# Expert stages of a hybrid convolution and attention network: GpSimd waits after every eighth indirect transfer instead of every fourth

## The chip, the cores and the metric

The kernel runs on one core of a Trainium2 chip. The metric is the device time of one launch in microseconds (us), the median of several runs. A core has five engines that run their own instruction streams and meet at semaphores: TensorE (PE, matrix products), VectorE (DVE), ScalarE (ACT), GpSimd (POOL) and SyncE (SP, here a queue for plain transfers). Sixteen DMA engines move data between the core's memory and the chip's main memory.

## What is computed

Eight images of 128 channels and 32x32 pixels, 8192 tokens of 128 numbers, pass through six layers: convolutional attention, whitening, linear attention, a mixture of experts with GELU, windowed attention, and a mixture of experts with SiLU. The change touches the two mixtures. Both pick two of eight experts for each token:

```python
def _L2_ffn_ref(x, Wr, br, ln_g, ln_b, W1, b1, W2, b2):      # "gelu"
    logits = xt @ Wr + br
    top_p, top_idx = jax.lax.top_k(jax.nn.softmax(logits, axis=-1), 2)
    weights = top_p / top_p.sum(axis=-1, keepdims=True)
    ...                                   # xe: normalised xt, scaled for each expert
    h = jax.nn.gelu(jnp.einsum('end,edh->enh', xe, W1) + b1[:, None, :], approximate=False)
    y = jnp.einsum('enh,ehd->end', h, W2) + b2[:, None, :]
    ...                                   # sel: the two chosen experts' rows of y
    out = (weights[:, :, None] * sel).sum(axis=1)

def _L3_ffn_ref(x, router_w, w1, w2, w3):                     # "silu"
    ...                                   # gates: the two largest probabilities, normalised
    h = jax.nn.silu(h1) * h3              # h1 = flat @ w1, h3 = flat @ w3, for each expert
    out = jnp.einsum('ne,nec->nc', gates, jnp.einsum('neh,ech->nec', h, w2))

t = t + _L2_ffn_ref(_ln_t(t), ...)
t = t + _L3_attn_ref(_ln_t(t), ...)
t = t + _L3_ffn_ref(_ln_t(t), ...)
```

## The kernel before

The layers run one after another, with a barrier of all engines between them. `tokens` (128 partitions x 64 tiles x 128) stays in the core's memory the whole time. A tile is 128 tokens.

A mixture is done in two parts. `route` scores the tokens, picks their two experts and gives each of the 64 x 128 x 2 token copies a row number (`places`), so that in main memory the rows of one expert stand together. `run_experts` (L1358) then moves the rows and multiplies them; it is called once with the prefix `g`/`gx` (gelu) and once with `s`/`sx` (silu).

The tiles are cut into four groups of 8, 24, 24 and 8 (`GROUP_TILES`). Each group has its own buffers in main memory and is sorted by itself into units of 256 rows, 15, 31, 31 and 15 of them (`GROUP_UNITS`), 92 in all. Four streams work on them:

- GpSimd first sends all four groups, then fetches all four (L1437 to L1440). `send_group` (L1413) issues, for each tile, two indirect transfers of 128 rows of 512 bytes each from `normed` to `sorted_rows` (L1416). `fetch_group` (L1422) waits until the group's results are stored, and then fetches parts of four tiles (`SEND`), eight indirect transfers each (L1430), into one of two buffers `fetch`. Counted through, there are 16 parts, numbered 0 to 15: parts 0 and 1 belong to group 0, 2 to 7 to group 1, 8 to 13 to group 2, and 14 and 15 to group 3. From the third part on, it waits before a part until VectorE has added the part two before it (`fetch_used`).
- SyncE loads a unit into `xq` (L1450) and stores a result `yq` (L1456). Before the first unit of a group it waits for all the group's sends: `sp.wait_ge(sent[g], 2 * GROUP_TILES[g] * 16)`.
- TensorE, ScalarE and VectorE run in steps, one unit per step and 96 steps in all: transpose of unit s (`turned`, L1496), first product of unit s-2 (`up`, L1471 to L1473), second product of unit s-4 (`down`, L1506). VectorE copies the weights of the unit's expert into `w_now` in each step (a cast, L1557).
- VectorE adds the fetched rows to `tokens` (`add_result`, L1587 to L1594): tiles of parts 0 and 1 in steps 50 to 57, those of parts 2 to 7 in steps 62 to 85, one tile a step, and the tiles of parts 8 to 15 after the last step. Before the first tile of a part it waits until the whole part has landed (`fetched`).

The order is fixed by the code; no planner is involved. A wait that GpSimd makes holds back everything behind it in its stream. The next layer's instructions follow a barrier that comes after the last addition.

## Time and profile before

| what | value |
|---|---|
| median of 3 runs | 1896.82 us (1893.26 to 1902.1) |
| the profiled execution | 1900.54 us |
| its span, first to last instruction | 1898.8 us |
| TensorE busy | 1268.0 us, 67% |
| VectorE busy | 1126.8 us, 59% |
| GpSimd busy | 807.7 us, 43% |
| GpSimd L1416, sends, 256 transfers | 142.5 us busy (silu) and 128.1 us (gelu) |
| GpSimd L1430, fetches, 256 transfers | 134.8 us busy (silu) and 124.2 us (gelu) |

Busy shares are averages over layers with different limits; what one layer waits for is read in its own stretch. A busy entry of GpSimd for an indirect transfer is the time in which the engine writes the transfer's descriptors; the move itself happens afterwards. The number in brackets behind a row in order of time is how long the engine had been idle, with what released it. In the gelu mixture `run_experts` lies between 572 and 1077 us of the span, in the silu mixture between 1384 and 1878 us.

### The profile page before, as it was taken

What the parts mean: (1) busy time and instruction counts of PE and PEld (TensorE: products, weight loads), DVE (VectorE), ACT (ScalarE), POOL (GpSimd) and SP (SyncE); (2) the same over time, 40 slices, a digit from 0 to 9 for tenths busy, and PEclk for the clock granted to TensorE, in tenths of its full rate; (3) what the DMA queues carried; (4) which work ended last, traced back from release to release, by engine and by line L of the source; (5) the groups of instructions that cost most, each with busy time, mean ns of one, the idle gap of its engine ahead of it and who ended that gap; (6) DMA issues with size and microseconds to landing.
All of it is one profiled execution on the core that took longest, in us unless ns stands there. A gap on an engine that the chain in (4) does not pass through costs nothing. (4 is left out here: it accounts for less than half of the span.)

```text
span 1898.8 us, 34652 instructions
## 1 busy us (share of the span) xinstructions
PE 1268.0 (67%) x12312; PEld 1135.5 (60%) x12312; DVE 1126.8 (59%) x2515; ACT 581.8 (31%) x1223; POOL 807.7 (43%) x717
## 2 busy tenths in 40 slices
PE   3878877356742769899980067766528599999702
PEld 2656557356732768898980045545518599999702
DVE  3999984998761323445541376855626277888612
ACT  2666651021211324445440042324102133333201
POOL 4666650222505655523535410104056666445353
PEclk9899997689556979999995578965559799999956
DMA  9100000000202233323321100003012233333212
GB/s 358 40 18 22 1 1 3 3 1 9 92 0 67 73 101 107 101 88 95 104 73 40 34 2 4 4 3 89 0 56 77 92 108 109 101 99 103 67 39 111
DMA packets 90575, 118.34 MB, mean 62 GB/s; under 512 B 18882, under 2 KB 74170, under 8 KB 90426
## 3 DMA queue, kind: packets, MB, share of 16 engines
q1 hardware_dynamic: 70842, 70.66, 11.8%
q0 software_dynamic: 19584, 45.65, 7.5%
q8 instruction: 99, 1.62, 0.4%
q14 instruction: 50, 0.41, 0.1%
HBM read 59.10 MB, written 57.15 MB: 61 GB/s over the span
## 5 line engine op out<-in xcount | busy, mean ns | idle before, releaser
L199 POOL TENSOR_TENSOR probs_low<-probs,probs_high 128x1024 fp32r<-128x1024 f32 x64 | 152.6, 2387 | 111.2 <-ACT probs_high L387 111.2
L1430 POOL DMA_INDIRECT gx_fetch<-sorted_results,g_places x128 | 124.2, 970 | 164.5 <-DVE tokens L1594 87.3
L1416 POOL DMA_INDIRECT sorted_rows<-s_normed,s_places x128 | 142.5, 1113 | 119.7 <-DMA sorted_rows<-s_normed,s_places 49.6
L1430 POOL DMA_INDIRECT sx_fetch<-sorted_results,s_places x128 | 134.8, 1053 | 134.1 <-DMA sx_fetch<-sorted_results,s_places 51.9
L1506 PE MATMUL gx_down<-g_w_down,gx_hT 128*128 x1472 | 183.6, 279 | 0.2 <-issue 0.2
L1416 POOL DMA_INDIRECT sorted_rows<-g_normed,g_places x128 | 128.1, 1001 | 125.7 <-DMA sorted_rows<-g_normed,g_places 55.0
L1506 PEld LDWEIGHTS gx_down<-g_w_down,gx_hT 128*128 128x128 f32 x1472 | 175.8, 196 | 0.8 <-issue 0.6
L1531 ACT ACTIVATE gx_hT<-gx_up,gx_b_now 128x256 f32<-128x256 f32 x368 | 144.1, 483 | 3.6 <-PE gx_down L1506 3.6
L1506 PE MATMUL sx_down<-s_w_down,sx_hT 128*128 x1104 | 140.6, 277 | 3.6 <-issue 2.1
L1506 PEld LDWEIGHTS sx_down<-s_w_down,sx_hT 128*128 128x128 f32 x1104 | 131.6, 193 | 6.0 <-issue 5.8
L1471 PE MATMUL gx_up<-gx_xT_high,gx_w_now 128*128 128x256 f32 x368 | 112.0, 304 | 31.2 <-issue 19.2
L1524 ACT ACTIVATE sx_xT_high<-sx_turned 128x256 fp32r<-128x256 f32 x92 | 35.4, 385 | 313.3 <-PE sx_down L1506 250.4
L1524 ACT ACTIVATE gx_xT_high<-gx_turned 128x256 fp32r<-128x256 f32 x92 | 35.5, 386 | 261.8 <-PE gx_down L1506 174.2
L1473 PE MATMUL gx_up<-gx_xT_high,gx_w_now 128*128 128x256 f32 x368 | 104.8, 285 | 0.0
L1472 PE MATMUL gx_up<-gx_xT_low,gx_w_now 128*128 128x256 f32 x368 | 104.7, 285 | 0.0
L1556 DVE COPY gx_b_now<-g_up_bias 128x4 f32 x92 | 17.4, 189 | 139.6 <-ACT gx_hT L1531 78.7
L1557 DVE CAST sx_w_now<-s_w_up 128x1368 fp32r x92 | 80.8, 879 | 29.4 <-issue 29.4
L384 ACT ACTIVATE probs<-score,nmax 128x1024 f32<-128x1024 f32 x64 | 71.4, 1115 | 81.4 <-DVE nmax L306 69.2
L1471 PEld LDWEIGHTS gx_up<-gx_xT_high,gx_w_now 128*128 128x128 f32 x368 | 70.6, 192 | 39.8 <-issue 39.6
L1585 DVE COPY sx_yq<-sx_down 128x256 f32<-128x256 f32 x92 | 39.0, 424 | 85.0 <-PE sx_down L1506 82.1
L1583 DVE TENSOR_TENSOR gx_yq<-gx_down,g_down_bias 128x256 f32<-128x256 f32 x92 | 38.7, 421 | 85.2 <-PE gx_down L1506 71.4
L1496 PE MATMUL sx_turned<-ident,sx_xq 128*128 128x128 f32 x184 | 35.9, 277 | 75.3 <-DMA sx_xq<-sorted_rows 74.2
(408 smaller groups left out, 3643.6 us busy)
## 6 DMA issues: line engine op xcount, KB each, us to landing
gx_xq<-sorted_rows SPq DMA_DIRECT2D x92, 128.0 KB
sorted_results<-gx_yq SPq DMA_DIRECT2D x92, 128.0 KB
sx_xq<-sorted_rows SPq DMA_DIRECT2D x92, 128.0 KB
sorted_results<-sx_yq SPq DMA_DIRECT2D x92, 128.0 KB
sorted_rows<-zeros POOLq DMA_DIRECT2D x20, 512.0 KB, 16.2
xin<-in_x SPq DMA_DIRECT2D x8, 512.0 KB, 3.6
feats<-in_x SPq DMA_DIRECT2D x1, 4096.0 KB, 29.8
out<-plane SPq DMA_DIRECT2D x8, 512.0 KB, 2.6
```

Source lines behind the costliest of these rows:

```text
L199: pool.tensor_tensor(probs_low[i][:, :], probs[i][:, :], probs_high[i][:, :].bitcast(F32), ALU.subtract).then_inc(low_ready, 1)
L384: act.activation(probs[n % 4][:, :], score[n % 2][:, :], ACT.Exp, bias=nmax[n % 4][:, 0:1], accum_out=zsum[n % 4][:, 0:1]).then_inc(exp_do ...
L1416: pool.indirect_dma_start(out=sorted_rows[g], out_offset=bass.IndirectOffsetOnAxis(ap=places[:, at, r:r + 1], axis=0), in_=normed[:, at, : ...
L1430: pool.indirect_dma_start(out=fetch[n % 2][:, i, r, :], out_offset=None, in_=sorted_results[g], in_offset=bass.IndirectOffsetOnAxis(ap=pla ...
L1471: pe.matmul(out, left[:, part, columns], right[0][:, :], start=True, stop=False)
L1472: pe.matmul(out, left[:, part, columns], right[1][:, :], start=False, stop=False)
L1473: pe.matmul(out, left[:, part + 1, columns], right[0][:, :], start=False, stop=True)
L1506: done = pe.matmul(down[u % 2][:, P * k:P * k + C], hT[u % 2][0:width, i, P * k:P * k + P], w_down[0:width, bass.ds(e, 1), i, :].rearrange ...
L1524: act.activation(xT[u % 2][0][:, :], turned[u % 2][:, 0:UNIT], ACT.Copy).then_inc(x_high, 1)
L1531: done = act.activation(hT[i][:, k, :], up[i][k // 2][:, k % 2, :], ACT.Gelu, bias=b_now[i][:, k:k + 1])
L1557: dve.tensor_copy(w_now[i][:, :, :].rearrange("p m h -> p (m h)"), w_up[:, bass.ds(e, 1), :, :].rearrange("p a m h -> p (a m h)")).then_in ...
L1585: dve.tensor_copy(yq[u % 4][:, :, :], product).then_inc(y_ready, 1)
```

## The change

After every second tile that it sends, and after every second tile of a part that it fetches, GpSimd waited until all transfers issued so far in the group or part had landed. It now does so after every fourth tile. The counts waited for are as before at the places that remain. Between two such waits stand eight transfers in place of four. In each mixture 16 of 32 waits go in the sends and 16 of 32 in the fetches. The waits of the other engines are the same.

```diff
@@ send_group(g), run for each of the four groups
                         pool.indirect_dma_start(
                             out=sorted_rows[g], out_offset=bass.IndirectOffsetOnAxis(ap=places[:, at, r:r + 1], axis=0),
                             in_=normed[:, at, :], in_offset=None).then_inc(sent[g], 16)
-                    if at % 2 == 1:
+                    if at % 4 == 3:
                         pool.wait_ge(sent[g], (at + 1 - FIRST_TILE[g]) * 2 * 16)
@@ fetch_group(g), run for each of the four groups
                                 in_offset=bass.IndirectOffsetOnAxis(ap=places[:, n * SEND + i, r:r + 1], axis=0)
                                 ).then_inc(fetched[n % 2], 16)
-                        if i % 2 == 1:
+                        if i == SEND - 1:
                             pool.wait_ge(fetched[n % 2], (n // 2 * SEND + i + 1) * 2 * 16)
```

On GpSimd, at the start of `run_experts` (gelu), before (-) and after (+). 3840x128 is the buffer of group 0, 7936x128 that of group 1; `ladded` is the name under which the semaphore of group 0's sends (`sent[0]`) is printed, `gx_sent1` that of group 1's:

```order
 L1411 UNCONDITIONAL_BRANCH [waits barrier_Pool_Activation_PE_DVE_SP_gather]
-L1416 DMA sorted_rows<-g_normed,g_places 3840x128 x4
+L1416 DMA sorted_rows<-g_normed,g_places 3840x128 x8
 L1416 DMA sorted_rows<-g_normed,g_places 3840x128 [waits ladded]
-L1416 DMA sorted_rows<-g_normed,g_places 3840x128 x3
-L1416 DMA sorted_rows<-g_normed,g_places 3840x128 [waits ladded]
-L1416 DMA sorted_rows<-g_normed,g_places 3840x128 x3
-L1416 DMA sorted_rows<-g_normed,g_places 3840x128 [waits ladded]
-L1416 DMA sorted_rows<-g_normed,g_places 3840x128 x3
+L1416 DMA sorted_rows<-g_normed,g_places 3840x128 x7
 L1416 DMA sorted_rows<-g_normed,g_places 7936x128 [waits ladded]
```

Nothing moves past anything else: the same transfers stand in the same order, with two of the group's four waits gone.

On GpSimd, the last two parts that the gelu mixture fetches (14 and 15), before:

```order
L1430 DMA gx_fetch<-sorted_results,g_places 128x128 [waits gx_y_stored2,gx_y_stored3,gx_y_stored1,gx_fetch_used,gx_y_stored0,gx_fetched1]
L1430 DMA gx_fetch<-sorted_results,g_places 128x128 x3
L1430 DMA gx_fetch<-sorted_results,g_places 128x128 [waits gx_fetched0]
L1430 DMA gx_fetch<-sorted_results,g_places 128x128 x3
L1430 DMA gx_fetch<-sorted_results,g_places 128x128 [waits gx_fetch_used,gx_fetched0]
L1430 DMA gx_fetch<-sorted_results,g_places 128x128 x3
L1430 DMA gx_fetch<-sorted_results,g_places 128x128 [waits gx_fetched1]
L1430 DMA gx_fetch<-sorted_results,g_places 128x128 x3
```

and the same two parts now:

```order
L1430 DMA gx_fetch<-sorted_results,g_places 128x128 [waits gx_y_stored2,gx_y_stored3,gx_y_stored1,gx_fetch_used,gx_y_stored0,gx_fetched1]
L1430 DMA gx_fetch<-sorted_results,g_places 128x128 x7
L1430 DMA gx_fetch<-sorted_results,g_places 128x128 [waits gx_fetch_used,gx_fetched0]
L1430 DMA gx_fetch<-sorted_results,g_places 128x128 x7
L1375 UNCONDITIONAL_BRANCH [waits gx_fetched1]
```

The wait in the middle of each part is gone; the one at its end, and the waits for VectorE (`fetch_used`) and for the stored results, stand where they stood.

## Rows read from the trace of the kernel before

**Rows 1.** Busy time by stage (`stretch, PE, PEld, DVE, ACT, POOL busy (instructions), PEclk, DMA share, GB/s`).
```profile
572.00:598.00 26.00, 0.00 (x0) 0.00 (x0) 0.00 (x0) 0.00 (x0) 16.17 (x17) 0.50 0.12 40
598.00:678.00 80.00, 47.29 (x374) 45.30 (x374) 21.91 (x56) 26.04 (x68) 49.52 (x49) 0.82 0.25 77
996.00:1077.00 81.00, 0.00 (x0) 0.00 (x0) 16.91 (x54) 0.00 (x0) 45.65 (x48) 0.50 0.15 39
1410.00:1492.00 82.00, 51.34 (x414) 49.89 (x414) 36.05 (x67) 17.07 (x42) 51.22 (x49) 0.81 0.22 75
1797.00:1878.00 81.00, 0.00 (x0) 0.00 (x0) 17.06 (x55) 0.00 (x0) 45.65 (x48) 0.50 0.14 39
```

**Rows 2.** TensorE in order of time (`start us, us, engine line op out<-in xcount [idle before <-releaser]`): where it resumes.
```profile
599.22 1.11 PE L1496 MATMUL gx_turned<-ident,gx_xq 128*128 128x128 f32 x4 [45.68 <-DMA gx_xq<-sorted_rows]
...
678.60 0.69 PE L1496 MATMUL gx_turned<-ident,gx_xq 128*128 128x128 f32 x2 [24.37 <-DMA gx_xq<-sorted_rows]
...
1411.26 0.69 PE L1496 MATMUL sx_turned<-ident,sx_xq 128*128 128x128 f32 x2 [46.48 <-DMA sx_xq<-sorted_rows]
...
1493.23 0.69 PE L1496 MATMUL sx_turned<-ident,sx_xq 128*128 128x128 f32 x2 [27.70 <-DMA sx_xq<-sorted_rows]
```

**Rows 3.** SyncE's queue in order of time: the first load of group 1, gelu.
```profile
676.58 0.32 SPq L1450 DMA_DIRECT2D gx_xq<-sorted_rows  x1
```

**Rows 4.** GpSimd in order of time: sends of groups 0 and 1, gelu.
```profile
573.41 0.99 POOL L1416 DMA_INDIRECT sorted_rows<-g_normed,g_places  x1 [0.30 <-issue]
...
578.46 0.95 POOL L1416 DMA_INDIRECT sorted_rows<-g_normed,g_places  x1 [1.54 <-DMA sorted_rows<-g_normed,g_places]
...
631.85 0.96 POOL L1416 DMA_INDIRECT sorted_rows<-g_normed,g_places  x1 [1.87 <-DMA sorted_rows<-g_normed,g_places]
...
670.56 0.95 POOL L1416 DMA_INDIRECT sorted_rows<-g_normed,g_places  x1 [1.52 <-DMA sorted_rows<-g_normed,g_places]
...
676.83 0.96 POOL L1416 DMA_INDIRECT sorted_rows<-g_normed,g_places  x1 [1.53 <-DMA sorted_rows<-g_normed,g_places]
```

**Rows 5.** GpSimd in order of time: fetches at the end of the gelu experts.
```profile
996.24 0.98 POOL L1430 DMA_INDIRECT gx_fetch<-sorted_results,g_places  x1 [21.42 <-DVE tokens L1594]
...
1002.86 0.94 POOL L1430 DMA_INDIRECT gx_fetch<-sorted_results,g_places  x1 [1.84 <-DMA gx_fetch<-sorted_results,g_places]
...
1009.36 0.94 POOL L1430 DMA_INDIRECT gx_fetch<-sorted_results,g_places  x1 [1.82 <-DMA gx_fetch<-sorted_results,g_places]
...
1072.09 0.94 POOL L1430 DMA_INDIRECT gx_fetch<-sorted_results,g_places  x1 [0.30 <-issue]
```

**Rows 6.** VectorE in order of time: additions of the last part, gelu.
```profile
1074.69 2.69 DVE L1594 SCALAR_TENSOR_TENSOR tokens<-gx_fetch,g_gates,tokens 128x128 f32<-128x128 f32 x8 [10.38 <-DMA gx_fetch<-sorted_results,g_places]
```

**Rows 7.** GpSimd in order of time: sends, silu.
```profile
1416.32 0.96 POOL L1416 DMA_INDIRECT sorted_rows<-s_normed,s_places  x1 [2.06 <-DMA sorted_rows<-s_normed,s_places]
...
1491.32 0.96 POOL L1416 DMA_INDIRECT sorted_rows<-s_normed,s_places  x1 [1.52 <-DMA sorted_rows<-s_normed,s_places]
```

**Rows 8.** GpSimd in order of time: fetches at the end of the silu experts.
```profile
1797.68 0.98 POOL L1430 DMA_INDIRECT sx_fetch<-sorted_results,s_places  x1 [19.88 <-DVE tokens L1594]
...
1817.37 0.94 POOL L1430 DMA_INDIRECT sx_fetch<-sorted_results,s_places  x1 [1.95 <-DMA sx_fetch<-sorted_results,s_places]
```

**Rows 9.** The line of the 24 zero fills: durations in ns, then landing.
```profile
L192 POOL DMA_DIRECT2D sorted_rows<-zeros x24: 531/531/730, 3.3 to 15.6; - x24
...
DMA to landing us min/median/max: 3.3/17.0/35.9
```

**Rows 10.** The line of the sends, 572 to 598 us: landing.
```profile
DMA to landing us min/median/max: 2.2/2.2/2.4
```

**Rows 11.** Busy time of the first 4 us of sending (columns as in Rows 1).
```profile
572.00:576.00 4.00, 0.00 (x0) 0.00 (x0) 0.00 (x0) 0.00 (x0) 3.08 (x4) 0.50 0.10 33
```

**Rows 12.** VectorE and GpSimd in order of time, silu, beside one another.
```profile
1544.76 0.87 DVE L1557 CAST sx_w_now<-s_w_up 128x1368 fp32r x1 [0.32 <-issue]
...
1544.90 1.57 POOL L1416 DMA_INDIRECT sorted_rows<-s_normed,s_places  x1 [0.30 <-issue]
```

## The prediction

> **What bounds the kernel now.** I read the busy time by stage first, then TensorE in order of time, then GpSimd. TensorE is the busiest engine overall, so the question is where in `run_experts` it or VectorE stands still for GpSimd.
>
> There are three such stretches in each mixture. At the start, from 572 to 598 us, no compute engine does anything while GpSimd sends group 0 [rows 1]; TensorE resumes at 599.22 (gelu) and 1411.26 (silu) when the first unit has been loaded [rows 2]. Then TensorE finishes group 0 and stands for 24.37 us (gelu) and 27.70 us (silu) until group 1's first unit is there [rows 2]. That load is issued at 676.58 [rows 3], just as the last wait of group 1's sends ends and GpSimd goes on at 676.83 [rows 4]: the sends of group 1 are what is late. The third stretch is the end, 996 to 1077 and 1797 to 1878 us: TensorE and ScalarE show nothing, VectorE is busy 17 of 81 us, GpSimd issues 48 fetches [rows 1]. VectorE stands 10.38 us for the last part and adds it in 2.69 us [rows 6].
>
> Between group 1's start and the last step TensorE waits for no load (the two waits for a load in each mixture are those of rows 2), so there GpSimd's waits are off the path.
>
> **What one removed wait is worth.** GpSimd leaves 0.30 us between two issues even with no wait in between [rows 4]. After every fourth send it idles 1.5 to 1.9 us instead [rows 4], once 2.06 in silu [rows 7]. So a removed wait gives back its idle time less 0.30.
>
> *Sends, gelu.* The first unit of group 1 comes after 64 sends (16 of group 0, 48 of group 1), which have 16 waits. The 8 removed ones are every second, from the one that ends at 578.46 (1.54) to the one at 670.56 (1.52), with 1.87 the longest [rows 4]. The eight add up to 12.83 us; less 8 x 0.30 that is 10.4. Two of them lie in group 0, so TensorE begins 2.5 us earlier, and group 1 is there 10.4 us earlier: TensorE's second wait goes from 24.37 to 24.37 - 10.4 + 2.5 = 16.4 us. It stays well above nothing, so all 10.4 us are on the path. **10.4 us.**
>
> *Sends, silu.* The same 8 of 16 waits, seven of them at 1.52 or 1.53 and one at 2.06 [rows 7]: 12.7 - 2.4. TensorE's 27.70 us become some 20. **10.3 us.**
>
> *Sends of groups 2 and 3.* Another 8 waits in each mixture. GpSimd is through with them earlier, but TensorE already finds those units loaded: nothing on the path. The cover is group 1's 31 steps.
>
> *Fetches while the steps run* (parts 0 to 9). Before part 2 and from part 4 on GpSimd mostly waits for VectorE's additions, which are tied to step numbers; it will only wait longer there. VectorE never stands for a part in that stretch. **0.**
>
> *Fetches at the end.* Parts 8 and 9 are in the two buffers when the steps end. Part 10 starts when VectorE has added part 8 (996.24, after 21.42 us of idle time [rows 5]; 1797.68 in silu [rows 8]), so six parts, 10 to 15, are fetched at GpSimd's own pace, some 13.1 us each (from 996.24 to 1009.36 [rows 5]). In the middle of each stands one wait that goes: 1.84 in part 10 [rows 5], 1.75 to 1.95 elsewhere (1.95 is in silu's part 11 [rows 8]). The six add up to 10.78 us in gelu and 10.99 in silu; less 6 x 0.30, **9.0 and 9.2 us**. What is next in line there? VectorE's additions take 2.69 us a part, against a new pace of 11.6; and the part two before is added long before its buffer is wanted. The wait at each part's end, and the last landing with its additions, stay.
>
> **Sum:** 10.4 + 10.3 + 9.0 + 9.2 = 38.9 us. The profiled execution had 1900.54 us (span 1898.8), 3.7 over the median; taken off the median, 1896.82 - 38.9 = 1857.9, so **1858 us** (the execution with a profile some 1862).
>
> **The unknown: eight transfers in flight.** The trace has no indirect transfer issued behind more than three others without a wait. Two bounds. From below: the 24 fills with zeros at the start go out on the same queue of GpSimd with no wait between them. Their issue stays at 531 ns in the median, 730 at most, while landings take up to 35.9 us [rows 9], so many are outstanding and none holds up the next: cost 0. From above, the issue of an indirect transfer when something hinders it: 1.57 us, against 0.96 otherwise [rows 12], 0.61 more each. I take 0, since sends land 2.2 us after their issue [rows 10] and are issued 1.26 us apart, so that two at a time are under way whether four or eight go out; in the first 4 us 33 GB/s, or 132 KB, two transfers of 64 KB, had been moved, at a DMA share of 0.10 [rows 11]. The queue keeps up.
>
> **A hindrance that is already there.** The issue at 1544.90 took 1.57 us beside VectorE's cast at 1544.76, which took 0.87 [rows 12]; its neighbours take 0.96. While group 1 is sent, group 0's 15 units are computed, with 15 casts. The 49 issues of that stretch took 49.52 us in gelu and 51.22 in silu [rows 1]; at 0.96 each they would be 47.0, so 2.5 and 4.2 us went to such meetings. GpSimd now issues for a larger share of that time and a wait no longer swallows a cast. If all 15 casts cost 0.61 in each mixture, that is 9.15 - 2.5 and 9.15 - 4.2, together 11.6 us less gain. I take 0 for the forecast, since a meeting falls away elsewhere as often as one comes new, and keep 11.6 as a bound. At the end of a mixture VectorE runs no such cast.
>
> The Trainium skill has this as a rule that speaks against the change: in "SBUF — State Buffer", section "SBUF: two separate sides", a transfer issued by GpSimd stalls beside a VectorE copy in its fast mode, since GpSimd can't write descriptors meanwhile; its section "A bandwidth-pool intuition that's wrong (but worth ruling out)" gives 620 ns alone against some 3100 beside. The trace agrees on the kind, at 0.61 us and not 2.5. By the page's pair, an estimate, the 19 meetings that 11.6 / 0.61 stands for would cost 47 us, and the change would lose. It is rival 1 below, at another price.
>
> **The rivals.**
> 1. *Casts take part of the gain.* As above, at the row's price: 1858 + 11.6 = **1870 us**. For it: silu already pays 4.2 us. Against: TensorE is idle, without casts, for the last 24 to 28 us of those sends.
> 2. *The waits only merge.* If transfers drained more slowly than they are issued, the wait after eight would be twice the one after four, and nothing would be gained: **1897 us**. Against it are rows 10 and 11, and the equal idle times of 1.5 us whatever stood before.
> 3. *Only one of the two stretches is on the path*, since something I don't see releases TensorE or the additions: 1897 - 19 or 20 = **1878 us**. Rows 3 and 4 tie the first, rows 5 and 6 the second.
> 4. *Slower: an issue behind more than four unlanded ones is hindered.* Place: transfers five to eight of each batch, 8 batches of sends and 6 parts in each mixture, 28 in the kernel that count. At 0.61 us for each of four issues, a batch costs 2.44 and gains 1.39 (38.9 / 28): 28 x 1.05 = 29 us, **1926 us**. It decides from 0.35 us per issue, where the gain is gone. Against: no more than two are ever outstanding [rows 10], and the fills [rows 9].
> That the change does not do what it says is excluded for GpSimd's stream: the order of the built program has half the waits.
>
> **How the numbers follow.** Forecast 1858: 0.80. Rival 1: 0.09. Rival 2: 0.06. Rival 3: 0.03. Rival 4: 0.02. A measurement of this kernel can tell some 0.5%, 9.5 us, from no change. Forecast and rivals 1 and 3 are faster by more than that: 0.92. Rival 2 is the same: 0.06. Rival 4 is slower: 0.02. The range: the runs of before lie 4 us below and 5 above their median, so 1858 may read from 1850 on; upwards it takes in rival 1, 1870. More is not needed, since 0.11 is left out.
>
> **What the profile after would show.** Behind each eighth send an idle time of about 1.5 us, behind the others 0.30; from the start of the first send to the first of group 2 in the gelu mixture 94.4 us in place of 104.8 (the second send starts at 573.41, 1.4 after the first, and group 2's first at 676.83 [rows 4]); TensorE's second wait at 16.4 and 20; the last six parts 11.6 us apart; VectorE's idle time before each part down from 10.4 to 8.9. Wrong it would be if the idle time after eight were 2.8 or more (rival 2), if fetches or sends took longer from the fifth on (rival 4), if the 49 issues took over 55 us (rival 1), or if TensorE's second wait kept its length while the sends got shorter (rival 3).

## The result, and the profile after

The change made the kernel **slower**: 2030.28 us in the median of four runs (2020.04 to 2039.69), against 1896.24 us for the kernel before (1893.26 to 1902.1). The ratio is 1.070, with a 95% interval of 1.063 to 1.077. Forecast were 1858 us and a range of 1850 to 1870. The profiled execution took 2039.69 us, 139 us more than that of the kernel before.

GpSimd does exactly what was forecast. GpSimd in order of time, gelu sends, in the kernel after (columns as in [rows 4]):

```profile
580.07 0.95 POOL L1416 DMA_INDIRECT sorted_rows<-g_normed,g_places  x1 [1.53 <-DMA sorted_rows<-g_normed,g_places]
...
660.75 0.96 POOL L1416 DMA_INDIRECT sorted_rows<-g_normed,g_places  x1 [0.30 <-issue]
663.24 0.96 POOL L1416 DMA_INDIRECT sorted_rows<-g_normed,g_places  x1 [1.52 <-DMA sorted_rows<-g_normed,g_places]
```

The idle time behind eight sends is 1.52, as it was behind four [rows 4], and an issue still takes 0.96. Group 2's first send starts at 663.24, 94.7 us after the first of all; forecast were 94.4, and before it was 104.8. At the end of the gelu experts a part of eight fetches follows the last one after 11.6 us, the forecast number, in place of 13.1 [rows 5]:

```profile
1097.73 0.94 POOL L1430 DMA_INDIRECT gx_fetch<-sorted_results,g_places  x1 [1.85 <-DMA gx_fetch<-sorted_results,g_places]
...
1109.30 0.94 POOL L1430 DMA_INDIRECT gx_fetch<-sorted_results,g_places  x1 [1.85 <-DMA gx_fetch<-sorted_results,g_places]
```

The time is lost where the prediction put a nought: **in the steps that are computed beside the sends and fetches.** Busy time of three stretches of the gelu experts, first of the kernel before and then of the one after (columns as in [rows 1]). Each time they are steps 15 to 36 (beside sends), 36 to 55, and 55 to 91 (beside fetches), from ScalarE's first operation of the one step to that of the other:

```profile
683.00:768.00 85.00, 77.19 (x632) 75.22 (x631) 32.82 (x84) 38.74 (x106) 49.46 (x50) 0.97 0.32 104
768.00:843.00 75.00, 69.84 (x574) 68.25 (x575) 33.20 (x87) 34.83 (x95) 27.78 (x28) 0.98 0.30 93
843.00:982.00 139.00, 128.81 (x1084) 125.67 (x1083) 72.14 (x199) 66.76 (x182) 60.82 (x62) 1.00 0.33 96
```
```profile
670.00:817.00 147.00, 106.05 (x636) 96.84 (x635) 33.71 (x86) 39.02 (x107) 72.15 (x75) 0.75 0.23 72
817.00:886.00 69.00, 67.33 (x569) 65.72 (x568) 32.05 (x86) 34.68 (x95) 1.93 (x3) 1.00 0.24 75
886.00:1071.00 185.00, 148.96 (x1077) 141.60 (x1076) 71.57 (x199) 65.57 (x180) 60.11 (x62) 0.88 0.25 72
```

The same instructions, and VectorE and ScalarE are busy as long as before, but the first stretch takes 62 us more and the third 46 more. The middle one, in which GpSimd now issues nearly nothing (3 instructions), takes 6 less. Silu shows the same: 43 and 37 us more beside sends and fetches (80 to 123, 134 to 171), 1 less between. What was forecast as gain is there as well: 10 to 11 us up to step 15 in each mixture, 9 at each tail. Together 188 - 7 - 21 - 18 = 142, of 139 measured.

What do the steps wait for? ScalarE's waits in the kernel before, then in the one after (`engine line waited for: us in total, times, longest us`). L1524 is ScalarE's first operation of a step; it waits for the increment of `stepped` that TensorE attaches to the last matmul of the step:

```profile
ACT gx_xT_high L1524 <- PE gx_down L1506: 174.2, 70, 29.3
...
ACT gx_xT_high L1524 <- remote: 12.5, 3, 4.7
```
```profile
ACT gx_xT_high L1524 <- PE gx_down L1506: 153.7, 53, 12.4
ACT sx_xT_high L1524 <- remote: 141.7, 24, 7.4
ACT gx_xT_high L1524 <- remote: 138.9, 20, 9.6
```

"remote" is what the profile writes when it finds no instruction that ended shortly before the wait did. In the kernel before that is 12.5 us in gelu and nothing in silu; after, it is 281 us. One such wait, in the silu sends, TensorE first, then ScalarE and GpSimd:

```profile
1578.73 0.50 PE L1506 MATMUL sx_down<-s_w_down,sx_hT 128*128 x3
1578.98 0.36 PE L1471 MATMUL sx_up<-sx_xT_high,sx_w_now 128*128 128x256 f32 x1
...
1581.09 0.27 PE L1473 MATMUL sx_tails<-sx_xT_high,sx_w_now 128*85 128x256 f32 x1
1584.84 0.41 PE L1496 MATMUL sx_turned<-ident,sx_xq 128*128 128x128 f32 x2 [3.48 <-DVE sx_xT_low L1565]
```
```profile
1583.85 0.38 ACT L1524 ACTIVATE sx_xT_high<-sx_turned 128x256 fp32r<-128x256 f32 x1 [7.18 <-remote]
```
```profile
1572.31 0.96 POOL L1416 DMA_INDIRECT sorted_rows<-s_normed,s_places  x1 [1.53 <-DMA sorted_rows<-s_normed,s_places]
...
1581.78 0.95 POOL L1416 DMA_INDIRECT sorted_rows<-s_normed,s_places  x1 [0.30 <-issue]
1584.26 0.96 POOL L1416 DMA_INDIRECT sorted_rows<-s_normed,s_places  x1 [1.53 <-DMA sorted_rows<-s_normed,s_places]
```

The matmul that carries the increment is over at 1579.23. TensorE goes on with the next step's products, so here it is not held up itself (deeper in a run it is; see the sends by sixteen). But ScalarE, VectorE (1583.86) and SyncE (1583.85) all see the step's end only at 1583.85, 4.6 us late: when the run of eight transfers is over and lands. The trace's record of the semaphore itself says the same: the increment stands at 1583.83, the landing of the last transfer at 1583.82 to 1584.00. Before that TensorE had run out of work at 1581.4. I call this a **late increment** below.

The records of three profiled executions of the changed kernel (this one and two of the experiments) give, by where in a run of eight a step's last matmul ended, how many of the next steps began over 0.6 us late (0.04 us is usual):

```
ended in a run, us after its first issue    steps   late
0 to 3                                        65       5
3 to 11                                      214     161
11 and more, in the wait for the landing       17       0
in no run of transfers                       274       4
```

The example is not the rule for the end of a hold. Counted by the first engine that waits, 26 of the 56 late increments of the first profile come 1.9 to 2.6 us after the start of the run's last issue, which is its landing; 25 come earlier, while the run still goes on, and 8 are held past a landing into the next run.

A step may run ahead by about one: a hold of 2 us is mostly hidden, one of 5 us is not. TensorE also loses clock on the way: from 735 to 758 us two steps of 11.5 us each ran at a granted clock of 0.58, mostly at the lower of its two levels (1.2 of 2.4 GHz), after ScalarE and with it TensorE had been kept waiting for 9.6 us at a time; TensorE was busy for 14.74 of 23 us. In the two stretches above with a mean clock of 0.75 and 0.88 the same matmuls are busy for 28.9 and 20.2 us more than before; in the one at 1.00 they are not. Over the whole kernel its busy time rose from 1268.0 to 1351.9 us with the same 12312 instructions. How much of the loss is the clock's and how much the waiting alone, no run separates.

```profile
735.00:758.00 23.00, 14.74 (x61) 12.90 (x60) 3.32 (x8) 3.68 (x10) 15.62 (x17) 0.58 0.20 68
```

### The profile page after: what moved, and what is told of

It reads as the page before. It is cut to its first block and busy times, and to the rows that moved or that the text cites. A ratio compares the mean times of both kernels' runs of the same rounds, so it can differ in the third digit from the quotient of the medians.

```text
span 2037.9 us, 34652 instructions
## 1 busy us (share of the span) xinstructions
PE 1351.9 (66%) x12312; PEld 1194.8 (59%) x12312; DVE 1126.1 (55%) x2515; ACT 580.9 (29%) x1223; POOL 787.1 (39%) x717
## 3 DMA queue, kind: packets, MB, share of 16 engines
q0 software_dynamic: 19584, 45.65, 7.0%
## 5 line engine op out<-in xcount | busy, mean ns | idle before, releaser
L1506 PE MATMUL gx_down<-g_w_down,gx_hT 128*128 x1472 | 210.0, 296 | 21.4 <-issue 20.2
L1430 POOL DMA_INDIRECT sx_fetch<-sorted_results,s_places x128 | 128.3, 1002 | 231.5 <-DVE tokens L1594 184.8
L1506 PEld LDWEIGHTS gx_down<-g_w_down,gx_hT 128*128 128x128 f32 x1472 | 195.6, 210 | 31.1 <-issue 30.5
L1416 POOL DMA_INDIRECT sorted_rows<-s_normed,s_places x128 | 130.5, 1019 | 99.0 <-POOLq L1091 40.9
L1506 PE MATMUL sx_down<-s_w_down,sx_hT 128*128 x1104 | 156.0, 295 | 15.7 <-issue 14.2
L1471 PE MATMUL gx_up<-gx_xT_high,gx_w_now 128*128 128x256 f32 x368 | 120.8, 328 | 62.5 <-DVE gx_w_now L1557 43.5
L1506 PEld LDWEIGHTS sx_down<-s_w_down,sx_hT 128*128 128x128 f32 x1104 | 143.4, 207 | 23.8 <-issue 23.5
L1524 ACT ACTIVATE sx_xT_high<-sx_turned 128x256 fp32r<-128x256 f32 x92 | 35.3, 384 | 380.2 <-PE sx_down L1506 181.4
L1583 DVE TENSOR_TENSOR gx_yq<-gx_down,g_down_bias 128x256 f32<-128x256 f32 x92 | 38.9, 423 | 182.3 <-remote 105.3
L1524 ACT ACTIVATE gx_xT_high<-gx_turned 128x256 fp32r<-128x256 f32 x92 | 35.5, 386 | 355.9 <-PE gx_down L1506 153.7
L1471 PEld LDWEIGHTS gx_up<-gx_xT_high,gx_w_now 128*128 128x128 f32 x368 | 78.4, 213 | 73.1 <-issue 73.0
L1473 PE MATMUL gx_up<-gx_xT_high,gx_w_now 128*128 128x256 f32 x368 | 113.6, 309 | 3.3 <-issue 3.2
L1472 PE MATMUL gx_up<-gx_xT_low,gx_w_now 128*128 128x256 f32 x368 | 113.1, 307 | 1.4 <-issue 1.4
## 6 DMA issues: line engine op xcount, KB each, us to landing
feats<-in_x SPq DMA_DIRECT2D x1, 4096.0 KB, 29.9
```

The source lines that it names most:

```text
L1416: pool.indirect_dma_start(out=sorted_rows[g], out_offset=bass.IndirectOffsetOnAxis(ap=places[:, at, r:r + 1], axis=0), in_=normed[:, at, : ...
L1430: pool.indirect_dma_start(out=fetch[n % 2][:, i, r, :], out_offset=None, in_=sorted_results[g], in_offset=bass.IndirectOffsetOnAxis(ap=pla ...
L1471: pe.matmul(out, left[:, part, columns], right[0][:, :], start=True, stop=False)
L1472: pe.matmul(out, left[:, part, columns], right[1][:, :], start=False, stop=False)
L1473: pe.matmul(out, left[:, part + 1, columns], right[0][:, :], start=False, stop=True)
L1506: done = pe.matmul(down[u % 2][:, P * k:P * k + C], hT[u % 2][0:width, i, P * k:P * k + P], w_down[0:width, bass.ds(e, 1), i, :].rearrange ...
```

## The experiments

Theory A, from these traces: a run of indirect transfers that GpSimd issues without a rest holds back TensorE's increments until it is over; what counts is its length, and whether steps are computed beside it. Its rivals: only a landing wait lets them through (A2), a common cause such as the lower clock (B), the number of transfers on their way (C). The kernels of one comparison ran on the same chip, with the kernel before beside them. There were five comparisons, on chips that I call P, Q, R (twice) and S; on which chip the result above was measured isn't known. Ratios are to the kernel before of the same comparison, with 95% intervals.

### The two halves, on chip P

Sends by eight, fetches by four:

```
-                    if at % 2 == 1:
+                    if at % 4 == 3:
                         pool.wait_ge(sent[g], (at + 1 - FIRST_TILE[g]) * 2 * 16)
```

> One part of the change alone: the sends wait after every eighth, the fetches after every fourth as before. Theory A (a run of transfers issued without a rest holds back the increments that TensorE attaches to its last matmul of a step, until the run is over; what counts is how long a run is and whether steps are computed beside it): from the start of step 15 to that of step 36, beside the sends of groups 1 and 2, the changed kernel took 62 us more than before in gelu and 43 in silu, and some 16 to 18 us less up to step 15 and from 36 to 55 together, +77 in all; the fetches go back to what they were, so 1896 + 77 = 1973 us. ScalarE's waits that are put down to 'remote' are seen up to step 36 and no longer beside the fetches. Rival B (sends and fetches share one cause that needs both, as a lower clock of TensorE through the whole mixture): the time lies nearer to 1896 or nearer to 2030 than to the middle.

Fetches by eight, sends by four:

```
-                        if i % 2 == 1:
+                        if i == SEND - 1:
                             pool.wait_ge(fetched[n % 2], (n // 2 * SEND + i + 1) * 2 * 16)
```

> The other part alone: sends after every fourth as before, fetches after every eighth. Theory A: beside the fetches (step 55 to 91) the changed kernel took 46 us more in gelu and 37 in silu, and 9 less in each tail: 1896 + 65 = 1961 us. The two parts add up to the whole: (1973 - 1896) + (1961 - 1896) = 142 against the measured 134. Rival B: as for the first part alone; the parts then don't add up. The prediction's own picture (fetches beside steps cost nothing) would give 1896 - 18 = 1878.

Both expectations failed, and in a way that no theory had foreseen. The kernel before took 1875.36 us here, not 1896. Sends by eight: **1852.6 us, 0.988 (0.985 to 0.991)**. Fetches by eight: **1856.01 us, 0.990 (0.987 to 0.992)**. Both were *faster*, by 22.8 and 19.4 us, where the prediction's sum had 20.7 for the sends and 18.2 for the fetches. ScalarE's waits of the first one:

```profile
ACT gx_xT_high L1524 <- PE gx_down L1506: 181.9, 88, 20.2
ACT sx_xT_high L1524 <- PE sx_turned L1496: 50.3, 3, 44.4
```

There is no wait put down to "remote". In the records no step is late by over 0.6 us, though 32 runs of eight are sent and steps end in all parts of them. On this chip there are no late increments.

### A rest in place of the wait, and waits for older transfers, on chip P

GpSimd fills a tile of its own where each removed wait stood:

```
                     if at % 4 == 3:
                         pool.wait_ge(sent[g], (at + 1 - FIRST_TILE[g]) * 2 * 16)
+                    elif at % 2 == 1:
+                        rests.append(0)
+                        pool.memset(rest[:, :], 0.0).then_inc(rested, 1)
+                        pool.wait_ge(rested, len(rests))
...                       # and the same in fetch_group
```

> The changed kernel, with a pause where each removed wait stood: GpSimd fills a tile of its own with zeros (1280 numbers in each of 128 partitions, some 1.2 us by the 0.95 us that 1024 take) and waits for that alone, not for a landing. Theory A in its plain form (a rest in the issuing is what lets the increments through): like the kernel before, 1890 to 1905 us, steps beside sends back to 3.5 to 4 us. Rival A2 (it needs a wait for the landing itself, by its semaphore): still some 2030 to 2040. Rival B (the lower clock): no view.

Waits for the tile before, from two semaphores by turns:

```
-                    if at % 2 == 1:
-                        pool.wait_ge(sent[g], (at + 1 - FIRST_TILE[g]) * 2 * 16)
+                    tile = at - FIRST_TILE[g]
+                    if tile >= 1:
+                        pool.wait_ge(sent[g][(tile - 1) % 2], ((tile - 1) // 2 + 1) * 2 * 16)
+                    if tile % 4 == 3:
+                        pool.wait_ge(sent[g][tile % 2], (tile // 2 + 1) * 2 * 16)
```

> Sends alone, fetches as before. After each tile (two transfers) GpSimd waits for the landing of the tile before it, which has landed already or nearly (a send lands 2.2 us after its issue, two are issued in 2.5), and after every eighth for all. So there are never more than four on their way, as in the kernel before, but GpSimd runs on for eight. Theory A (length of the run without a rest): no better than the sends by eight alone, some 1973 us. Rival C (the number on their way counts): like the kernel before less the sends' gain, 1876 to 1896 us.

Measured: the rest 1878.32 us, 1.002 (1.000 to 1.004); the older waits 1860.41 us, 0.992 (0.989 to 0.995). With nothing held back on this chip they couldn't tell the theories apart. They give the prices without late increments, and were run again below.

### The change again, shorter runs, longer runs, and runs only where engines idle, on chip Q

> The changed kernel itself, once more. The runs of its two halves showed no late increments of TensorE at all and gained 22.8 and 19.4 us over a kernel before that took 1875 there in place of 1896. Theory A' (the holding back of TensorE's increments behind a run of transfers is not there on every chip; it is a property of the chip or of how the program lies on it): where the kernel before takes some 1875 us and its ScalarE shows no wait put down to 'remote', the change gives the sum of its halves, 1875 - 42 = 1833 us (the prediction's 38.9 us less would be 1836); where the kernel before takes some 1896 us, it gives some 2030 us again. Rival D (the loss needs both halves at once, on any chip): 1990 us or more although the kernel before takes 1875.

**2057.34 us, 1.078 (1.069 to 1.087)**, beside a kernel before of 1906.48. ScalarE shows 172.7 us of "remote" in gelu and 148.6 in silu. So in one comparison the late increments are there and in another they aren't, and where they are the kernel before is slower too. Rival D is not refuted by this run, but by the halves on chip R below.

A wait after each tile, that is every second transfer (`if True:` in both places):

> The other way: GpSimd waits for landing after every second transfer, in sends and fetches. In place of one idle time of 1.24 us per eight transfers that the change takes away, this adds one per four on the path: 16 sends' waits and 12 fetches' waits in each mixture, 56 x 1.24 to 1.4 = 69 to 78 us more than before where nothing is held back: 1875 + 74 = 1949 us. Where increments are held back (kernel before 1896), a run of two is too short to hold one for long, so that the 21 us that before loses there come back: again some 1949 us, and no wait put down to 'remote'.

**2001.53 us, 1.050 (1.044 to 1.056).** No wait is put down to "remote", on a chip that shows 321 us of them with runs of eight: that part held. The time was 52 us over the expectation. The sum had only GpSimd's pace in it. GpSimd gets to its first fetch at 824 us (786 before), and VectorE's additions, tied to step 50, stand in its queue for it. What stands behind them is the next step's input; TensorE's waits in this kernel:

```profile
PE sx_turned L1496 <- DVE sx_xT_low L1565: 23.9, 4, 17.8
```

Silu's steps 36 to 55 took 91 us in place of 71, and its steps 55 to 91 took 144 in place of 134.

Runs of eight only for group 0, the last 16 sends of group 1 and parts 10 to 15; four elsewhere:

```
-                    if at % 2 == 1:
+                    if at % 4 == 3 or (at % 2 == 1 and FIRST_TILE[1] <= at < FIRST_TILE[2] - 8 or at >= FIRST_TILE[2] and at % 2 == 1):
...
-                        if i % 2 == 1:
+                        if i == SEND - 1 or (i % 2 == 1 and n < 10):
```

> Runs of eight only where no step is computed beside them: group 0's 16 sends, the last 16 of group 1 (TensorE stands for them), and the fetches of parts 10 to 15; runs of four elsewhere. Gain on any chip, by the prediction's own rows: two waits in group 0, two in group 1, six in the tail, 10 x 1.3 = 13 to 14 us in each mixture, 27 us together: 1875 - 27 = 1848, or 1896 - 27 = 1869 where increments are held back (theory A). By theory D or any in which eight in flight cost by themselves, it would lose there too.

**1876.63 us, 0.985 (0.979 to 0.991)**: 29.9 us less, 27 expected. Here the prediction's arithmetic holds on a chip that shows late increments, as long as no step is computed beside the long runs.

Sends by sixteen (`if at % 8 == 7:`), fetches by four:

> Sends with a wait after every sixteenth transfer, fetches by four as before. Theory A': where nothing is held back, 4 waits more go of the 64 transfers ahead of group 1's first unit, so 5 to 6 us less in each mixture than the sends by eight: 1852.6 - 11 = 1842 us. Where increments are held back, a run of sixteen lasts some 20 us and holds a step for up to 15: beside the sends of groups 1 and 2 most steps would take a good part of a run, clearly over the 1973 expected of sends by eight there.

**2088.87 us, 1.098 (1.091 to 1.105)**, the slowest of all, although its fetches go by four as before. ScalarE in order of time, beside the sends of the gelu experts:

```profile
645.31 1.56 ACT L1531 ACTIVATE gx_hT<-gx_up,gx_b_now 128x256 f32<-128x256 f32 x4
713.77 0.38 ACT L1524 ACTIVATE gx_xT_high<-gx_turned 128x256 fp32r<-128x256 f32 x1 [66.90 <-remote]
714.05 1.56 ACT L1531 ACTIVATE gx_hT<-gx_up,gx_b_now 128x256 f32<-128x256 f32 x4
751.73 0.38 ACT L1524 ACTIVATE gx_xT_high<-gx_turned 128x256 fp32r<-128x256 f32 x1 [36.11 <-remote]
```

The direction is theory A's, the size isn't. The matmul that carries the increment ended at 644.19, and ScalarE, after 66.9 us of standing still, saw it at 713.77, 69.6 us late. In that time GpSimd rested three times for a landing (its sends at 659.7, 681.2 and 702.6 stand behind waits), and none of the three let it through. So the end of a run doesn't always release an increment. Theory A as worded is too simple.

It is incomplete too, for TensorE didn't run on here. It spent the time from 648.55 to 709.93 on one step, which takes it 3.7 us at the full clock (760.69 to 764.37 in the same trace). TensorE in order of time, one matmul at a time, none of them waiting for a semaphore:

```profile
655.60 0.37 PE L1473 MATMUL gx_up<-gx_xT_high,gx_w_now 128*128 128x256 f32 x1 [1.72 <-issue]
...
706.76 0.37 PE L1506 MATMUL gx_down<-g_w_down,gx_hT 128*128 x1 [2.43 <-issue]
709.56 0.37 PE L1506 MATMUL gx_down<-g_w_down,gx_hT 128*128 x1 [2.43 <-issue]
```

I counted such idle times, over 0.2 us before a matmul for which nothing is waited, in the records of both mixtures of every run. Here there are 79, 113 us together; in the first profile of the changed kernel 42, 24 us together, 40 of them during a run of transfers; also in every other kernel with runs of eight beside steps on chips Q and R. There is none with runs of four or two beside steps, and none on chips P and S. So what is held up is first TensorE's increments and, where it goes on, TensorE's own matmuls.

### The four again on chip R, which shows late increments

> The changed kernel with a pause of some 1.2 us (a fill with zeros, waited for) where each removed wait stood; again, since increments were held back nowhere where it ran first. Where the kernel before takes some 1875 us this run says nothing new (it was 1878 beside 1875). Where it takes some 1900: theory A (the length of a run without a rest) gives a time within 10 us of before; rival A2 (only a wait for landing lets the increments through) gives 2030 to 2060, as the changed kernel.

> Sends with a wait, after each tile, for the landing of the tile before, and for all after every eighth transfer; fetches by four. Where the kernel before takes some 1900 us: theory A (length of the run) gives a time like that of the sends by eight beside it, 1970 to 2000; rival C (the number on their way counts) some 1885. Where it takes 1875: 1860 as the first time.

> Sends by eight, fetches by four, as the first time (0.9876 of before where nothing was held back). Where the kernel before takes some 1900 us, theory A gives before + 77 by the first profile of the changed kernel (its steps beside sends), up to before + 100 by its second: 1973 to 2006.

> Sends by four, fetches by eight (0.9898 of before where nothing was held back). Where the kernel before takes some 1900 us, theory A gives before + 52 to + 65 (steps 55 to 91 took 46 and 37 us longer in the first profile of the changed kernel, 45 and 25 in its second; 18 less in the two tails): 1948 to 1971. The two halves' differences add up to that of the whole change within some 15 us.

Beside a kernel before of 1908.2 us (columns: us, ratio with its interval, what it costs over the same kernel's difference on chip P, ScalarE's "remote" in gelu and silu):

```
rest in place of the wait   1919.9    1.010 (1.003 to 1.018)   11.7 -  3.0 =   9     63.6    8.7
waits for the tile before   1937.27   1.018 (1.010 to 1.026)   29.1 + 15.0 =  44     65.5   68.4
sends by eight              1994.71   1.049 (1.041 to 1.058)   86.5 + 22.8 = 109     96.2   87.5
fetches by eight            1969.09   1.034 (1.026 to 1.041)   60.9 + 19.4 =  80     73.2   60.5
```

The halves lose 86.5 and 60.9 us; together 147, and the whole change had lost 151 on chip Q. So they add up, and rival D and rival B fall: either half loses by itself, in its own stretch. A2 falls with the rest: 1919.9 us, where the changed kernel is over 2017 on every such chip. A fill of 1.2 us, with no landing waited for, does nearly all that the wait did. It isn't quite within the 10 us that I had set; the first difference alone is uncertain by 15 us either way, so I read nothing into the 9. What this run doesn't separate is the rest from an empty queue: from the end of one issue to the start of the next pass 1.47 us (0.28 and a fill of 1.19), a send lands 2.2 us after its start, and its issue takes 0.96, so all four transfers have landed when GpSimd goes on. Whether the issuing has to stop or the transfers have to be through, no run tells.

The older waits give neither answer. At most four transfers are on their way, and GpSimd runs on for eight as with sends by eight; rival C wanted 1885 us, theory A 1970 to 2000, measured were 1937. The length of a run isn't all: to stop for a wait that is already met, and lets GpSimd go on after the same 0.30 us, takes away more than half of the loss. The late steps fit in between, counted by the first engine that waits: 42 of up to 5.3 us, against 44 of up to 11.2 with sends by eight, 35 of up to 2.5 with the rest, and 23 of up to 2.3 on the same chip with landing waits after four wherever steps are computed.

### Data or issuing, one increment or all, on chip R once more

> The changed kernel, as the measure for the others of this comparison. Where the kernel before takes some 1875 us: 1836. Where it takes 1895 to 1910: 2030 to 2060.

2017.27 us, 1.063 (1.060 to 1.066), beside 1897.07: the measure for the next two.

A quarter of each row, in sends alone:

```
-                            out=sorted_rows[g], out_offset=bass.IndirectOffsetOnAxis(ap=places[:, at, r:r + 1], axis=0),
-                            in_=normed[:, at, :], in_offset=None).then_inc(sent[g], 16)
+                            out=sorted_rows[g].rearrange("n (q c) -> (n q) c", q=4),
+                            out_offset=bass.IndirectOffsetOnAxis(ap=places[:, at, r:r + 1], axis=0),
+                            in_=normed[:, at, 0:C // 4], in_offset=None).then_inc(sent[g], 16)
```

> The changed kernel, but each send moves only the first quarter of each row (128 bytes in place of 512), to places of its own; the rest of the rows stays zero, so three quarters of the experts' input are left out, and the amount of compute is the same. As many transfers and rows, a quarter of the data. If the data hold TensorE's increments: beside the sends ScalarE has no or few waits put down to 'remote', and the time falls by 50 to 100 us against the changed kernel. If the issuing does (128 rows each by GpSimd): the same waits of 5 to 10 us and the time within 20 us of the changed kernel's. Where nothing is held back on this chip, it tells nothing.

2020 and 2060 us (two executions; the trace is of the longer one), not less than the changed kernel. GpSimd's queue moved 33.06 MB in place of 45.65 (of the DMA queues, first the changed kernel on the same chip, then this one), and ScalarE's waits from 599 us to the last gelu send are as many and as long:

```profile
q0 software_dynamic: 19584, 45.65, 6.9%
```
```profile
q0 software_dynamic: 19584, 33.06, 5.4%
```
```profile
ACT gx_xT_high L1524 <- remote: 77.8, 10, 11.0
```
```profile
ACT gx_xT_high L1525 <- remote: 67.7, 10, 10.4
```

The same 19584 packets; an issue takes 0.958 us in the median in both. **It isn't the amount of data; it is what GpSimd does for each transfer, or the number of packets.** Which of the two, no run tells.

A second increment, before the step's end, for ScalarE:

```
                 if s < NU:
                     done = turn(s)
+                    if s >= TO_DOWN:
+                        done.then_inc(x_turned, 1)
...
-                act.wait_ge(stepped, s + 1)
+                if TO_DOWN <= s < NU:
+                    act.wait_ge(x_turned, s - TO_DOWN + 1)
+                else:
+                    act.wait_ge(stepped, s + 1)
                 if s < NU:
                     take_x_high(s)
+                if TO_DOWN <= s < NU:
+                    act.wait_ge(stepped, s + 1)
```

> The changed kernel; from step 4 on TensorE gives a second increment at the last matmul of the turned inputs, some 1.8 us before the end of the step, and ScalarE's first operation waits for that one. If every increment of TensorE is held during a run, ScalarE's waits for it are as long (put down to 'remote', 5 to 10 us) when they fall into a run's later part, and the time stays within 30 us of the changed kernel's. If only the one at the end of a step is held, ScalarE's first operation starts on time in every step and only VectorE's first one, which still waits for the step's end, is late. Where nothing is held back: some 1836 us or a little less.

The five executions took 1973.84 to 2028.41 us, the median 1996.46, 21 us less than the changed kernel. (The ratio on record, 1.044 with 1.039 to 1.049, leaves out the two longest.) The loss is still there. ScalarE's waits for the new increment (L1527), in the trace of the longest execution:

```profile
ACT sx_xT_high L1527 <- remote: 89.5, 24, 7.5
...
ACT gx_xT_high L1527 <- remote: 60.9, 17, 5.6
```

So it is late as well: both increments of a step are affected, not one place in it. ScalarE's increments aren't. In all 184 steps of the first profile VectorE's L1565, which waits for one, starts within 0.11 us of ScalarE's end or of its own last operation. Its waits for them in gelu come to the same 30.0 us, two waits at the start of the mixture, in the changed kernel on this chip and in a kernel on a chip without late increments (S, below):

```profile
DVE gx_xT_low L1565 <- ACT gx_xT_high L1524: 30.0, 2, 27.0
```

> Runs of eight only where no step is computed beside them. Ten waits of some 1.3 us in each mixture go from the path, wherever it runs: 25 to 30 us less than before (ratio 0.984 to 0.987), on a chip of either kind.

**1863.75 us, 0.984 (0.981 to 0.986)**: 33.3 us less, a little over the expected 25 to 30.

### Shorter runs beside steps, on chip S

```
-                    if at % 2 == 1:
+                    if at % 4 == 3 or (at % 2 == 1 and FIRST_TILE[1] <= at < FIRST_TILE[2] - 8) or at >= FIRST_TILE[2]:
...
-                        if i % 2 == 1:
+                        if i == SEND - 1 or (i % 2 == 1 and n < 10):
```

> Runs of eight where no step is computed beside them, runs of two for the sends of groups 2 and 3 (20 us more for GpSimd in each mixture, with none waiting for it), runs of four elsewhere. If late increments behind runs of four cost time: on a chip that shows them 5 to 15 us less than the version beside it with runs of four there. If they are hidden by the step of slack, or where nothing is held back: the same within 3 us, or a few us more if VectorE's first addition at step 50 comes to wait for the fetch that now starts 20 us later.

> Runs of eight only where no step is computed beside them, four elsewhere, as the measure for the kernel beside it: 25 to 30 us less than before, ratio 0.984 to 0.986 as the two times before.

Chip S shows no late increments; the kernel before took 1873.87. Runs of four beside steps: **1845.38 us, 0.984 (0.981 to 0.986)**. Runs of two for groups 2 and 3: 1874.04 us, 0.999 (0.997 to 1.002), the whole gain gone. I had allowed "a few us" for VectorE's first addition. It was 10.50 us in gelu, and TensorE stood for it; VectorE in order of time, then TensorE's waits:

```profile
821.58 0.74 DVE L1594 SCALAR_TENSOR_TENSOR tokens<-gx_fetch,g_gates,tokens 128x128 f32<-128x128 f32 x2 [10.50 <-DMA gx_fetch<-sorted_results,g_places]
```
```profile
PE sx_turned L1496 <- DVE sx_xT_low L1565: 13.4, 2, 12.3
PE gx_up L1471 <- DVE gx_xT_low L1565: 9.0, 1, 9.0
```

Whether shorter runs would help on a chip with late increments this comparison couldn't say.

## Why the prediction was wrong, point by point

- **What bounds the kernel, and what one removed wait is worth: right.** The two halves gained 22.8 and 19.4 us on chip P, where the sum had 10.4 + 10.3 for sends and 9.0 + 9.2 for fetches. Those two runs are each a half; the whole change was never run on a chip without late increments, so the sum of 38.9 us is borne out by 42.2 in two parts. In the slow trace itself the sends are 10 us shorter up to group 1 and each tail 9. TensorE's second wait is 8.19 us in gelu and 4.80 in silu, not 16.4 and 20, only because late increments had already drawn out group 0's steps.
- **"Fetches while the steps run: 0" and "Sends of groups 2 and 3: nothing on the path": these are the steps that failed.** They asked only who waits for GpSimd. On the chips of the loss, GpSimd's run of transfers acts on everyone who waits for TensorE. In the first profile that is 62 + 43 us beside sends and 46 + 37 beside fetches, 188 us where the sum had 0.
- **"The unknown: eight transfers in flight", cost 0 to 11.6 us: the bounds were taken from the wrong quantity.** All rows were issue times and landings of GpSimd's own transfers [rows 9 to 12], and these did stay: 0.96 us, 2.2 us. No row of the bound looked at the steps beside a run. The kernel before had one view that did: its 12.5 us of "remote" at ScalarE's L1524, three waits of up to 4.7 us, and in its records, counted by the first engine that waits, 13 gelu steps late by up to 2.4 us and 6 silu steps by up to 1.0, all beside runs of four. A wait for another engine's increment that comes late with no cause in sight was the trace's sign that runs hold back steps.
- **The rivals.** Rival 4 had the right sign and a wrong mechanism: it made issues longer. Rivals 1 to 3 didn't happen; the meetings with VectorE's cast are there (issues of up to 1.6 us), as in [rows 12], but GpSimd's busy time fell, from 807.7 to 787.1 us. The Trainium skill, "SBUF — State Buffer", section "SBUF: two separate sides", tells of GpSimd held up beside VectorE. The trace doesn't bear that out as the cause: the median issue is 0.958 us in a kernel that loses 120 us. The loss runs the other way, from GpSimd to TensorE's increments.
- **The chance of 0.02 for slower** rested on having looked at all who share the path. Whatever is not on the path by its waits was taken to be without effect.

What stays open. *By which way* GpSimd's issuing holds up TensorE's increments, no run shows; nor why one was late by 69.6 us across three rests, nor why TensorE's own matmuls stall, nor why a wait that is already met helps. *Why two chips show it and two don't* is open too; it was there in both comparisons on R, but no run tells the chip from the core or the place in memory that the program was given. The kernel before took 1875 and 1874 us on P and S, 1897 to 1908 on Q and R. That this difference comes from its own late increments is shown in part. The first profile's steps 15 to 91 take 24 us more (20 in gelu, 3 in silu) than the same steps, also by four, on chip S. On chip Q, where the kernel with long runs only beside idle engines takes 89.3 and 77.8 us for steps 15 to 36 of the two mixtures, runs of two, which have no late increments, take 77.1 and 77.9; on chip S the former takes 77.3 and 78.4. So in gelu the extra time goes when the late increments go. The run meant to use this met a chip without them.

**The version that came out of this**, long runs only where no step is computed beside them, beat the kernel before in all three comparisons: 1876.63 beside 1906.48, 1863.75 beside 1897.07, 1845.38 beside 1873.87 us, ratios 0.985, 0.984 and 0.984. On Q and R it also beat the changed kernel (2057.34 and 2017.27). On S the changed kernel wasn't run; by the two halves' gain on P, 42.2 us, an estimate, it would be the faster of the two on a chip without late increments.

## What to carry to other kernels

A wait whose result nobody needs may still do work: it broke up GpSimd's issuing, and without it other engines' increments came late. Before taking one out, look at every stretch in which the freed engine will now issue on end, and ask what is computed beside it, not only who waits for it; take it out first where nothing is, which here kept two thirds of the gain (28.5 us on chip S, of the 42.2 of both halves on P) without the loss. And a result from one chip can have the wrong sign on another: the same halves of this change gave 0.99 on one chip and 1.03 to 1.05 on the next.

## What the hardware showed

- **An increment attached to a matmul can come late by microseconds** while GpSimd issues indirect transfers: with runs of two never by over 0.6 us, of four up to 2.6 where all beside the steps are fours, of eight up to 13 (by the records), of sixteen 69.6. TensorE itself runs on at first, and in long runs is slowed as well: 61 us for a step of 3.7. The nearest thing in the Trainium skill is a warning in "VectorE: DVE Perf Modes", section "The TRN2 errata — SBUF-src ops pay a fixed extra latency per instruction", that increments at a high rate from one engine can deadlock another, and that kernels should space them. Here nothing deadlocked; that closely spaced activity of one engine delays the increments of another is what these traces show, and no run tells whether it is the same mechanism.
- **It is there on some chips and not on others**: no late increment in the six profiles of chips P and S together (twice ScalarE alone began a step 1.1 and 1.4 us late, with SyncE on time), 55 to 58 late steps in each of the three profiles of the changed kernel.
- **The amount of data doesn't matter**: with 33.06 MB in place of 45.65 in the same 19584 packets, the waits stayed.
- **A rest of 1.2 us without any landing wait** brings nearly all of it back: 1919.9 us, where the changed kernel took 2017 to 2057.
